# Limits on the transfers under way in the edge stage of a four-layer graph network

## What is computed

```python
src, dst = edge_index[0], edge_index[1]
msg = jax.nn.relu(x[src] + edge_attr)                  # 21,250 x 512, float32
agg = jax.ops.segment_sum(msg, dst, num_segments=x.shape[0])
h = x + agg
h = jax.nn.relu(h @ W1 + b1) @ W2 + b2
h = x + h
# batch norm over the nodes, then x = layernorm(x + h)
```

## Time and profile before

| what | value |
|---|---|
| median of 3 runs | 662.99 us (662.35 to 663.97) |
| profiled execution, span from its first to its last instruction | 713.5 us |
| mean granted TensorE clock in it | 0.872 |
| first and last gather start in it | 379.3 us, 635.8 us |
| busy in the span: PE, DVE, ACT, POOL | 72%, 57%, 34%, 44% |
| DMA: moved in all, mean over the span | 103.21 MB, 145 GB/s |

### The profile page before, as it was taken

One profiled execution on the slowest core, in us unless ns is written; L12 is line 12 of the kernel. 1 busy time (PEld: TensorE's weight loads), 2 busy tenths in 40 slices (PEclk: granted clock), 3 DMA queues, 4 the chain that ended last, 5 costly groups with the idle time before them and its releaser, 6 DMA issues.

```text
span 713.5 us, 8544 instructions
## 1 busy us (share of the span) xinstructions
PE 514.1 (72%) x2508; PEld 360.1 (50%) x2508; DVE 404.3 (57%) x942; ACT 241.1 (34%) x389; POOL 317.4 (44%) x359
## 2 busy tenths in 40 slices
PE   1587886998998999799980661808586817809976
PEld 1243332898888883699760110304243505505776
DVE  1599886466754859311572443735474836636357
ACT  1534455112055314511024332406252505315215
POOL 7468886900001203750005776672675664750000
PEclk9779999899999999899995666867988978958999
DMA  6700000000000210000939996996998979850003
GB/s 217 223 1 1 1 0 3 2 0 0 1 1 1 72 48 0 2 0 0 350 122 327 324 353 204 364 319 238 365 334 322 391 254 340 290 167 0 2 1 144
DMA packets 35655, 103.21 MB, mean 145 GB/s; under 512 B 6559, under 2 KB 7201, under 8 KB 35610
## 3 DMA queue, kind: packets, MB, share of 16 engines
q1 hardware_dynamic: 22170, 58.59, 22.6%
q0 software_dynamic: 13440, 44.05, 18.2%
HBM read 97.51 MB, written 5.12 MB: 144 GB/s over the span
## 4 chain that ended last, share of the span: by engine, by line
PE 44%; issue 15%; DVE 12%; another core or an unknown queue 8%; ACT 8%; POOL 7%; DMA 4%; DVEq 2%; POOLq 0%; ACTq 0%; SPq 0%
PE ps L1116 16%; PE ps L1141 8%; PE ps L1268 4%; PE ps L1236 4%; PE ps L1257 3%; DVE ea L963 3%; POOL xg L474 3%; POOL hot_lo L399 2%; ACT ea L629 2%; DVE stats L851 2%; DMA xg<-x_dram,srcT_i 2%; PE ps L1045 2%; PE ps L1181 2%; DVE xn L871 2%
## 5 line engine op out<-in xcount | busy, mean ns | idle before, releaser
L474 POOL DMA_INDIRECT xg<-x_dram,srcT_i x168 | 169.6, 1010 | 154.1 <-issue 110.8
L1236 PE MATMUL ps<-ea,hot_w 128*32 128x512 f32 x336 | 90.1, 724 | 84.9 <-ACT ea L629 76.9
L963 DVE TENSOR_TENSOR ea<-ea,xg 128x512 f32<-128x512 f32 x168 | 106.8, 685 | 21.3 <-DMA xg<-x_dram,srcT_i 16.7
L629 ACT ACTIVATE ea<-ea 128x2048 f32<-128x2048 f32 x42 | 79.8, 1910 | 45.5 <-DVE ea L963 36.6
L1236 PEld LDWEIGHTS ps<-ea,hot_w 128*32 128x32 f32 x336 | 17.0, 123 | 133.5 <-ACT ea L629 67.7
L978 DVE TENSOR_TENSOR x3T<-x3T,ps 128x128 f32 x84 | 24.2, 288 | 105.4 <-PE ps L1246 48.8
L399 POOL TENSOR_SCALAR hot_lo<-iota_n,lo_col 128x128 bf16<-128x128 f16 x84 | 56.8, 686 | 8.6 <-POOL lo_col L395 8.6
L1073 PE MATMUL ps<-hot_code,hot_lo 128*128 128x380 bf16 x168 | 38.5, 357 | 23.2 <-POOL hot_lo L399 12.5
L755 DVE TENSOR_SCALAR hot_code<-iota_n,codeT 128x380 bf16<-128x380 f16 x168 | 51.8, 368 | 3.9 <-issue 3.8
L1116 PE MATMUL ps<-counts,xs_hi 128*128 x120 | 44.6, 372 | 4.2 <-POOL xs_lo L438 4.2
L1116 PE MATMUL ps<-counts,u_hi 128*128 x120 | 44.0, 367 | 5.0 <-issue 5.0
(11 more groups left out here) (175 smaller groups left out, 993.0 us busy)
## 6 DMA issues: line engine op xcount, KB each, us to landing
ea<-in_edge_attr_dram SPq DMA_DIRECT2D x41, 1024.0 KB
w_s<-in_L_gnn_W_dram SPq DMA_DIRECT2D x5, 1024.0 KB, 11.8
xg<-x_dram,srcT_i POOLq DMA_INDIRECT x168
xn<-in_x_dram SPq DMA_DIRECT2D x3, 768.0 KB, 13.0
x_dram<-xn SPq DMA_DIRECT2D x9, 256.0 KB
out_dram<-xn SPq DMA_DIRECT2D x9, 256.0 KB
w_s<-in_L_gnn_W_dram SPq DMA_DIRECT2D x2, 512.0 KB, 9.2
b_b<-in_L_gnn_b_dram SPq DMA_DIRECT2D x3, 256.0 KB, 5.9
```

What stands on the lines that cost most here:

```text
L474: pool.indirect_dma_start(out=xg[:, slot, r, :], out_offset=None, in_=x3_dram[:, :], in_offset=bass.IndirectOffsetOnAxis(ap=srcT_i[:, r, g ...
L629: act.activation(ea[g % RING][:, :, :], ea[g % RING][:, :, :], ACT.Relu).then_inc(relu_done, 1)
L963: dve.tensor_tensor(ea[s][:, r, :], ea[s][:, r, :], xg[:, slot, r, :], ALU.add).then_inc(add_done, 1)
L1236: ins = pe.matmul(ps[at_w:at_w + EW, 4 + g // 2 % 2, :], hot_w[:, g % RING, 2 * b + r, :], ea[g % RING][:, 2 * b + r, :], start=(r == 0), ...
```

## The change

SyncE gets a second wait in front of each load from group 9 on: the load of group g is issued only once that of group g - 2 has landed. POOL gets a second wait in front of each gather from group 3 on: the gather of tile n is issued only once that of tile n - 5 has landed. Data, buffers, transfers and their order stay as they are.

```diff
 POOL_HOTS = 2
 HOTS = 4
 XRING = 3
+LOADS_OUT = 2
+GATHERS_OUT = 5
...
                 s = g % RING
                 if g >= RING:
                     sp.wait_ge(scat_done, g - RING + 1)
+                    sp.wait_ge(ea_loaded[(g - LOADS_OUT) % RING], 16 * ((g - LOADS_OUT) // RING + 1))
                 if g < NG - 1:
...
                 for r in range(TPG):
                     if g >= XRING:
                         pool.wait_ge(add_done, TPG * (g - XRING) + r + 1)
+                        pool.wait_ge(xg_loaded[(TPG * g + r - GATHERS_OUT) // TPG % XRING][(r - GATHERS_OUT) % TPG],
+                                     16 * ((TPG * g + r - GATHERS_OUT) // TPG // XRING + 1))
                     pool.indirect_dma_start(out=xg[:, slot, r, :], out_offset=None, in_=x3_dram[:, :],
```

## The result

The change makes the kernel slower by 4.7%: 692.6 us (median of 4 runs, 691.0 to 696.4) against 662.7 us (658.0 to 664.0), ratio 1.0471, 95% interval 1.0426 to 1.0516. I had forecast 666 us with a range of 657 to 673.

A forecast was written before the change was run, and what follows sets the result against it. The prediction took the edge stage as bound by two close ceilings, DMA (204 us) and POOL's issuing (210 us). Waits on loads and wait instructions at nothing plus 3 us for the gather's wait on 663.0 gave 666 us, range 657 to 673.

The forecast's parts named there:

- The 204 us of DMA and 210 us of issuing: Edge stage: DMA needs 81.7 MB at 401 GB/s, 204 us; POOL needs 168 gathers at 1.25 us, 210 us.
- Where the 50 us between the span and the median went: Edge stage: undisturbed runs lack most stalls; POOL's 43.2 us of waits matches the 50.5 us between span and median.
- The load's wait at nothing: SyncE's limit of two loads costs nothing; the ring of nine covers a hold of 2 us.
- The wait instruction at nothing: POOL's added wait, when already satisfied, costs nothing, hidden under the 0.95 us of the gather before.
- The gather's wait: POOL's limit of five holds gathers beside loads about 1.1 us, landings continue at 1.40 us; cost taken as 3 us.
- the prediction's main sum: Edge stage: 3 gathers of lost lead x 1.25 us = 3.8 us, taken as 3 us on the 663.0 us median.
- What is lost is the lead: POOL's lead over additions stays at five gathers instead of growing to eight, so the last nine groups run 3.8 us later.
- The bounds: Gather's wait: from 0, if stalls reset the lead, to 17 us, 116 contended gathers at 1.40 instead of 1.25 us.
- The rival "much slower": Contended gathers are released late and their queue runs dry now and then: 12 us, 675 us, chance 0.10.
- The rule on taking turns: DMA queues: a shallower load queue hands the gathers nothing, so the sum stays +3 us.
- The faster rival: Edge stage: POOL's pauses break ACT's stalls before they form, 655 us; chance 0.19 for 655 to 661.
- the 8 us: Faster rival's gain: two stalls like the 12.1 us wait spared in part, 4 us each, 663 to 655.

The follow-up runs named there:

- the profile beside 663 us: The kernel before, no edit, profiled on a chip where it takes about 663 us: 663.5 us beside 662.9.
- the limit of seven: Only POOL's wait added to the kernel before, with seven gathers allowed under way instead of five: 664.6 us, ratio 1.0036; beside about 712 us, 712.2.

## Why the prediction was wrong

*What bounds the kernel: right.* The 204 us of DMA and 210 us of issuing, one close above the other, are what an undisturbed execution shows: 224.8 us of issuing with DMA at 1.02 and 391 GB/s. The 210 us left out that a gather's own time grows beside loads, to 1.04 us on average. Where the 50 us between the span and the median went was an inference, and the profile beside 663 us bears it out in part: of the 52.8 us between the two spans, 31.7 lie in the issuing, where POOL's waits were, and 21.9 behind the last gather, which the prediction did not count.

*The load's wait at nothing: right,* ratio 0.9998 for the limit of two loads alone.

*The wait instruction at nothing: right within 2.4 us,* by the limit of seven.

*The gather's wait: the step that failed* is "of five gathers, about 2.2 lie in issue and completion (...), the others are queued, and the landings go on at 1.40 us". They did not go on: a gather lands every 1.60 us in place of 1.31, between 440 and 560 us. I took the fixed part of a gather's time and assumed that the rest was a full queue. But a gather that nothing holds needed 7.0 to 8.2 us to land, and five of them at 1.35 us are 6.7 us, so the fifth back was often still on its way. Seven are 9.4 us, and that limit held four gathers. Landings beside loads also come unevenly: POOL stops for 1 to 2 us, issues a few at 1.25 us, and stops again, and each stop ends 0.74 us after a landing, a delay that the prediction's main sum has at nothing. The mean under way is then 4.0, not 5, of the 5.2 to 6.1 that the stage has when it is free. The loads don't fill the hole: with the gathers' limit alone, each load was released by a scatter and so by the gathers themselves. DMA as a whole goes down to 330 GB/s. From there everything follows: 31 us of issuing, not 3.

*"What is lost is the lead" fell too.* The limit in the first half alone cost 11.4 us that were never won back.

*The bounds were too narrow.* The upper one, 17 us, came from the landing pace of the kernel before beside loads, 1.40 us. That is a pace without the limit; the limit's own effect on the pace is not in it. The rival "much slower" named the right mechanism, late releases and a gather queue that runs dry now and then, and its sign in the profile (GB/s of contended stretches below 390). By the packets from 440 to 560 us, the gathers' queue moved nothing for 1.0 us in the kernel before, for 6.7 us in the changed one and for 15.0 us with the limit of five alone. But I gave this rival 0.10 and two thirds of that bound.

*The rule on taking turns* (the Trainium skill, DMA: Bandwidth & Descriptors, Queues, rings and completion order). That an engine takes turns between rows that have work says nothing on a row that has none for a part of the time, and the rule was used as if both always had some. Both queues lost share over the 120 us, the gathers' from 52.6% to 47.2% and the loads' from 49.2% to 44.6%.

*The faster rival holds elsewhere.* Where ACT's long idle stretches exist, the limit of five removes most of them and the medians are 8.1 and 6.4 us lower, near the 8 us that I gave it. That it came near is partly luck, since the 8 us were taken from an execution of this sort and set against the 663 us of the other. Fewer gathers under way or POOL's pauses could both be the reason; limits of six to eight remove neither the stretches nor the 712 us. What causes the stretches, and why only some chips have them, stays open. No version beat the kernel before beside 663 us.

## What to carry to other kernels

A limit on transfers under way must be set against time from issue to landing divided by the pace that is needed, both under full load, and with room for unevenness and for the time that the release takes: here 5.2 to 6.1 on average, seven was nearly free and five cost 4.3%. A price for such a limit can't be taken from the landing pace of the kernel without it. And before a profile is used, its span is held against the timed runs: here they differed by 50 us, and a change that helps in the profile's state hurt in the other.

## What the runs showed of the hardware

The same kernel takes 663 us on some chips and 712 us on others, and the profile of 713.5 us has idle stretches of up to 20.3 us on ACT during which POOL goes on issuing gathers. A held indirect gather starts on POOL 0.74 us after the landing that it waited for; one that isn't held starts 0.30 us after the one before. An indirect gather of 0.262 MB beside loads takes, by an estimate from limits of three and of none, 1.9 us from issue to landing and about 1.0 us for each gather under way, itself counted.
